# Block attention with the maxima turned later, three query slots, the next layer's norm spread into it, and gathers issued in pairs

## The reference, cut to what matters

```python
x = x + tanh(g_xattn[1]) * block_attention(layernorm(x), ctx, ctx, Wq, Wk, Wv, Wo)   # layer 2
x = x + tanh(g_ffn[1]) * hard_mixture(layernorm(x), sel_w, sel_b, comp_w, comp_b)    # layer 3
x = x + tanh(g_xattn[2]) * mlstm(layernorm(x), ctx, ctx, ..., rpe, ..., itok)        # layer 4

# block_attention: 16 heads of 8 channels, softmax over each block of 64 keys by itself
scores = einsum('bhpqd,bhpkd->bhpqk', qg, kg) * scale
attn = softmax(scores, axis=-1)
ob = einsum('bhpqk,bhpkd->bhpqd', attn, vg)
out = segment_sum(ob, rows) @ Wo.T
# layernorm(x) = (x - mean(x)) / sqrt(var(x) + 1e-5) over the channels
# hard_mixture: comp_outputs of the component whose selection logit is the largest
# mlstm: pos_emb = rpe[hops], 128 x 128 indices into a table of rows
```

## Time and profile before

| | |
|---|---|
| Median of three runs | 976.05 us (968.55 to 978.45) |
| The profiled execution | 982.52 us, its span 980.7 us |
| TensorE busy | 827.3 us (84%) |
| VectorE busy | 637.8 us (65%) |
| ScalarE busy | 555.0 us (57%) |
| GpSimd busy | 297.5 us (30%) |

### The profile page before, as it was taken

One profiled execution on the slowest core, in us unless ns is written; L12 is line 12 of the kernel. 1 busy time (PEld: TensorE's weight loads), 2 busy tenths in 40 slices (PEclk: granted clock), 3 DMA queues, 4 the chain that ended last, 5 costly groups with the idle time before them and its releaser, 6 DMA issues.

```text
span 980.7 us, 14095 instructions
## 1 busy us (share of the span) xinstructions
PE 827.3 (84%) x5561; PEld 500.1 (51%) x5569; DVE 637.8 (65%) x983; ACT 555.0 (57%) x947; POOL 297.5 (30%) x253
## 2 busy tenths in 40 slices
PE   5899999998947767789995998986889878889775
PEld 1676777774412322335544955563568754444322
DVE  3886767662566577428878667873877335776667
ACT  4797878774624344434554344444668564676464
POOL 1123332331347677433313031205792003000003
PEclk9999999997967799989995997896899998999889
DMA  6210000007000000000000000014000000000001
GB/s 223 67 65 19 24 20 21 20 23 96 14 11 15 16 19 17 20 24 22 22 14 1 1 1 1 0 44 174 0 1 1 1 1 0 1 1 0 1 0 43
DMA packets 12849, 25.65 MB, mean 26 GB/s; under 512 B 3560, under 2 KB 4848, under 8 KB 12528
## 3 DMA queue, kind: packets, MB, share of 16 engines
q1 hardware_dynamic: 8688, 16.36, 5.8%
q0 software_dynamic: 4096, 8.40, 3.4%
HBM read 23.69 MB, written 1.05 MB: 25 GB/s over the span
## 4 chain that ended last, share of the span: by engine, by line
PE 58%; DVE 24%; ACT 13%; issue 3%; DMA 1%; SPq 0%; POOL 0%; DVEq 0%; ACTq 0%
PE ps L324 8%; PE ps L296 8%; PE ps L786 6%; PE ps L925 3%; DVE small L713 3%; PE ps L561 2%; PE ps L1277 2%; PE ps L199 2%; PE ps L583 2%; DVE big L1012 2%; PE ps L1247 2%; ACT nT L218 2%; ACT nT L219 2%; DVE small L722 2%; PE ps L961 1%
## 5 line engine op out<-in xcount | busy, mean ns | idle before, releaser
L866 POOL DMA_INDIRECT pe<-in_rpe,idx x128 | 130.2, 1017 | 260.4 <-DMA pe<-in_rpe,idx 212.0
L366 DVE TENSOR_TENSOR big<-l1f_w,big 128x512 f16<-128x512 f32 x128 | 87.4, 692 | 45.1 <-ACT big L353 42.9
L352 ACT ACTIVATE l1f_w<-ps,wcols 128x512 f32<-128x512 f32 x128 | 90.0, 703 | 32.8 <-PE ps L296 30.3
L296 PE MATMUL ps<-vx,big 128*128 128x512 f16 x384 | 94.5, 399 | 2.7 <-DVE nT L225 2.7
L324 PE MATMUL ps<-big 128*128 128x128 f16 x1536 | 92.6, 221 | 4.9 <-DVE big L366 4.9
L324 PEld LDWEIGHTS ps<-big 128*128 128x128 f16 x1536 | 89.9, 99 | 12.6 <-DVE big L366 5.5
L353 ACT ACTIVATE big<-ps,wcols 128x512 f16<-128x512 f32 x128 | 90.5, 707 | 0.0
L701 ACT ACTIVATE big<-ps 128x1024 f32<-128x1024 f32 x32 | 32.7, 1023 | 60.9 <-PE ps L559 60.7
L296 PEld LDWEIGHTS ps<-vx,big 128*128 128x128 f16 x384 | 38.1, 102 | 46.4 <-issue 8.6
L786 PE MATMUL ps<-nT,l1f_w 128*128 128x512 f32 x128 | 59.3, 607 | 2.2 <-DVE nT L225 2.2
L1542 POOL TENSOR_TENSOR big<-l1f_w,big 128x512 f16<-128x512 f32 x8 | 10.1, 1267 | 138.7 <-ACT big L1579 138.7
(11 more groups left out here) (309 smaller groups left out, 1851.4 us busy)
## 6 DMA issues: line engine op xcount, KB each, us to landing
big<-in_l0x_w SPq DMA_DIRECT2D x16, 256.0 KB, 4.3
pe<-in_l2f_w SPq DMA_DIRECT2D x16, 256.0 KB, 5.8
pe<-in_rpe,idx POOLq DMA_INDIRECT x128, 2.6
cT<-in_cT SPq DMA_DIRECT2D x1, 1024.0 KB, 8.4
l1f_w<-in_l1f_w SPq DMA_DIRECT2D x1, 1024.0 KB, 5.4
vx<-in_ctok SPq DMA_DIRECT2D x1, 1024.0 KB, 16.6
out_xT<-xT SPq DMA_DIRECT2D x4, 256.0 KB, 2.2
xT<-in_xT SPq DMA_DIRECT2D x1, 768.0 KB, 6.4
```

Source lines behind the costliest of these rows:

```text
L296: mm = te.matmul(bank(f), w16[:, e, a, f * 128:(f + 1) * 128], x16[:, c, b, :], start=(n == 0), stop=(n == 2))
L352: act.activation(h32[:, f, :], bank(f), ACT.Relu, bias=b, scale=1 / W_UP)
L366: dve.tensor_tensor(h16[:, k % 2, 1, f, :], h32[:, f, :], h16[:, k % 2, 0, f, :], SUB).then_inc(M0["lo"], 1)
L866: pool.indirect_dma_start(out=pe[:, v * D:(v + 1) * D], out_offset=None, in_=ins["rpe"], in_offset=bass.IndirectOffsetOnAxis(ap=idx[:, v:v ...
```

## The change

Four things are changed.

1. In the loop of layer 2 the turning of the maxima of b+1 moves from ahead of the second pass to behind it, to the end of the batch.
2. The queries have three slots instead of two (QS = 3). The reciprocal sums `rsum` move to another buffer to make room.
3. The norm of layer 3 is taken out of `pe_norm` and its like. Chunks 0, 1 and 2 are normed within layer 2: the centring at the head of batches 6, 10 and 14 (stage 0), the variance at the head of batches 7, 11 and 15 (stage 1), on TensorE behind the same wait for the reduction as the projections; ScalarE copies, squares and takes the root, and VectorE multiplies at the end of batches 7, 11 and 15. Chunk 3 is normed in steps 0 to 2 of layer 3, in which TensorE turns no positions; the turnings of these two steps come at the end. The last output projection uses bank 3.
4. Gathers wait only once for each call, not once for each row, so that those of layer 0 and of the tail go in pairs. Eight gathers move from behind layer 2 to ahead of its first keys.

```diff
-        KS, QS = 3, 2
+        KS, QS = 3, 3
...
+        def early_at(b):
+            c, stage = divmod(b - BC - 2, BC)
+            return (c, stage) if 0 <= c < NCH - 1 and stage < 2 else (None, None)
+
+        def pe_early_norm(te, b):
+            c, stage = early_at(b)
+            if stage == 0:
+                te.wait_ge(s_x, 2 * NCH + c + 1)
+                te.matmul(bank(0), centre_w, xT[:, cs(c)], start=True, stop=True).then_inc(s_cen, 1)
+            elif stage == 1:
+                te.wait_ge(s_sq, 3 * NCH + c + 1)
+                te.matmul(bank(0), mean_w, early, start=True, stop=True).then_inc(s_var, 1)
...
+        def act_early_norm(act, link, b):
+            c, stage = early_at(b)
+            if stage == 0:
+                act.wait_ge(s_cen, 3 * NCH + c + 1)
+                act.activation(nT[:, cs(c)], bank(0), ACT.Copy)
+                act.activation(early, bank(0), ACT.Square).then_inc(s_sq, 1)
+            elif stage == 1:
+                act.wait_ge(s_var, 3 * NCH + c + 1)
+                link(act.activation(early, bank(0), ACT.Ln, bias=eps5[:]))
+                act.activation(early, early, ACT.Exp, scale=-0.5).then_inc(s_rstd, 1)
+
+        def dve_early_norm(dve, b):
+            c, stage = early_at(b)
+            if stage == 1:
+                dve.wait_ge(s_rstd, 3 * NCH + c + 1)
+                dve.tensor_tensor(nT[:, cs(c)], nT[:, cs(c)], early, MUL).then_inc(s_norm, 1)
...
+                if early_at(b)[1] is not None:
+                    if b + 1 < B:
+                        te.wait_ge(A2["mx"], 3 * b + 4)
+                    pe_early_norm(te, b)
...
                 if 1 <= b <= B:
                     pe_values(te, b - 1)
-                if b + 1 < B:
-                    pe_maxima(te, b + 1)
...
+                if b + 1 < B:
+                    pe_maxima(te, b + 1)
...
         def pool_layer2(pool, link):
+            for v in range(IN_L0, IN_L1, 2):
+                pool_gather(pool, v, v + 2)
...
-            pe_norm(te, 3)
...
+                if k == 0:
+                    te.wait_ge(s_x, 3 * NCH)
+                    te.matmul(bank(6), centre_w, xT[:, cs(NCH - 1)], start=True, stop=True).then_inc(s_cen, 1)
+                elif k == 1:
+                    te.wait_ge(s_sq, 4 * NCH)
+                    te.matmul(bank(7), mean_w, nT[:, cs(NCH - 1)], start=True, stop=True).then_inc(s_var, 1)
+                else:
+                    if k == 2:
+                        te.wait_ge(s_norm, 4 * NCH)
+                    pe_turn_positions(te, k - 2)
+            for u in (PG // 2 - 2, PG // 2 - 1):
+                pe_turn_positions(te, u)
...
         def pool_gather(pool, v0, v1):
+            if v0:
+                pool.wait_ge(s_gather, 16 * v0)
             for v in range(v0, v1):
-                if v:
-                    pool.wait_ge(s_gather, 16 * v)
```

More of the change, by code:

```diff
@@ L514, in flamingo_kernel @@
         qT = nT[:].bitcast(f16).rearrange("p (c r n) -> p c r n", c=NCH, r=2)
-        KS, QS = 3, 2
-        qblk1 = work[:, 0:1024].bitcast(f16).rearrange("p (s r j q) -> p s r j q", s=QS, r=2, j=4)
-        mblk = work[:, 1024:1536].bitcast(bf16).rearrange("p (s j q) -> p s j q", s=2, j=4)
-        rsum = work[:, 1536:2048]
+        KS, QS = 3, 3
+        qblk1 = work[:, 0:1536].bitcast(f16).rearrange("p (s r j q) -> p s r j q", s=QS, r=2, j=4)
+        mblk = work[:, 1536:2048].bitcast(bf16).rearrange("p (s j q) -> p s j q", s=2, j=4)
+        rsum = sm(1536, 512)
+        early = sm(1024, 512)
         mpart = sm(512, 32).bitcast(bf16)
@@ L582, in pe_project @@
             for j in range(4):
-                mm = te.matmul(bank(0), l1x_w[:, (3 + j) * D:(4 + j) * D], on[:, c % 2, j, :, :], start=(j == 0), stop=(j == 3))
+                mm = te.matmul(bank(3 if c == NCH - 1 else 0), l1x_w[:, (3 + j) * D:(4 + j) * D], on[:, c % 2, j, :, :], start=(j == 0), stop=(j == 3))
             mm.then_inc(A2["y_ps"], 1)
@@ L641, in pe_layer2 @@
                             te.wait_ge(s_x, 2 * NCH + (b - BC - 1) // BC + 1)
+                        c, stage = early_at(b)
+                        if stage is not None:
+                            te.wait_ge(s_sq if stage == 0 else s_rstd, 3 * NCH + c + 1)
                     for part in range(4):
@@ L668, in pool_layer2 @@
                 if b:
-                    v = IN_L0 + 2 * (b - 1)
+                    v = IN_L1 + 2 * (b - 1)
                     pool_gather(pool, v, v + 1)
@@ L679, in pool_layer2 @@
                             qT[:, b // BC, :, b % BC * S:(b % BC + 1) * S]).then_inc(A2["qblk"], 1)
-            pool_gather(pool, IN_L0 + 2 * (B - 1), S)
+            for v in range(IN_L1 + 2 * (B - 1), S, 2):
+                pool_gather(pool, v, v + 2)
         def act_queries(act, c):
@@ L698, in act_layer2 @@
                     act_queries(act, (b + 2) // BC)
+                act_early_norm(act, link, b)
                 for u in range(2):
@@ L749, in dve_layer2 @@
                     dve.wait_ge(A2["y_ps"], c + 1)
-                    dve.scalar_tensor_tensor(xT[:, cs(c)], bank(0), gt[:, 2:3], xT[:, cs(c)], MUL, ADD).then_inc(s_x, 1)
+                    dve.scalar_tensor_tensor(xT[:, cs(c)], bank(3 if c == NCH - 1 else 0), gt[:, 2:3], xT[:, cs(c)], MUL, ADD).then_inc(s_x, 1)
                 if b + 1 < B:
@@ L761, in dve_layer2 @@
                     dve_reduce(dve, b + 2, 0)
+                dve_early_norm(dve, b)
         CW2 = 2 * CW
@@ L778, in pe_layer3 @@
                 n = NC - 1 - k % NC
+                if k == 0:
+                    te.wait_ge(s_norm, 3 * NCH + 2)
+                if k == NC:
+                    te.wait_ge(s_norm, 4 * NCH)
                 for w, first_bank, done in ((n, 0, "sel"), (NC + n, 4, "comp")):
@@ L788, in pe_layer3 @@
                     mm.then_inc(F3[done], 1)
-                pe_turn_positions(te, k)
+                if k == 0:
+                    te.wait_ge(s_x, 3 * NCH)
[5 more added lines that the diff above has]
+                    if k == 2:
+                        te.wait_ge(s_norm, 4 * NCH)
+                    pe_turn_positions(te, k - 2)
+            for u in (PG // 2 - 2, PG // 2 - 1):
+                pe_turn_positions(te, u)
         def picks(k):
@@ L795, in act_layer3 @@
         def act_layer3(act, link):
-            act_norm(act, link, 3)
+            last = nT[:, cs(NCH - 1)]
             for k in range(NC * NCH // 2):
@@ L803, in act_layer3, with act_turned @@
                                bias=col("l1f_comp_b", NC - 1 - k % NC)).then_inc(F3["cand"], 1)
-                for r in range(2):
-                    act.wait_ge(X4["peT_ps"], 2 * k + r + 1)
-                    act.activation(*turned(k, r), ACT.Copy).then_inc(X4["peT_act"], 1)
+                if k == 0:
+                    act.wait_ge(s_cen, 4 * NCH)
+                    act.activation(last, bank(6), ACT.Square).then_inc(s_sq, 1)
+                elif k == 1:
+                    act.wait_ge(s_var, 4 * NCH)
+                    link(act.activation(last, bank(7), ACT.Ln, bias=eps5[:]))
+                    act.activation(last, last, ACT.Exp, scale=-0.5).then_inc(s_rstd, 1)
+                else:
+                    act_turned(act, k - 2)
+            for u in (PG // 2 - 2, PG // 2 - 1):
+                act_turned(act, u)
+        def act_turned(act, u):
+            for r in range(2):
+                act.wait_ge(X4["peT_ps"], 2 * u + r + 1)
+                act.activation(*turned(u, r), ACT.Copy).then_inc(X4["peT_act"], 1)
         def dve_layer3(dve, link):
-            dve_norm(dve, 3)
             for k in range(NC * NCH // 2):
+                if k == 2:
+                    dve.wait_ge(s_rstd, 4 * NCH)
+                    dve.tensor_tensor(nT[:, cs(NCH - 1)], bank(6), nT[:, cs(NCH - 1)], MUL).then_inc(s_norm, 1)
                 b = col("l1f_sel_b", NC - 1 - k % NC)
@@ L859, in flamingo_kernel @@
         IN_L0 = PER_STEP * NCH * E
+        IN_L1 = IN_L0 + 8
         qhalf = big[:, 0:QR * NH2 // 2 * S].rearrange("p (r j v) -> p r j v", r=QR, j=NH2 // 2)
         def pool_gather(pool, v0, v1):
+            if v0:
+                pool.wait_ge(s_gather, 16 * v0)
             for v in range(v0, v1):
-                if v:
-                    pool.wait_ge(s_gather, 16 * v)
                 pool.indirect_dma_start(out=pe[:, v * D:(v + 1) * D], out_offset=None, in_=ins["rpe"],
```

## The result

The changed kernel took 999.04 us (median of four runs, 994.83 to 1003.4), the kernel before on the same chip 975.9 us: ratio 1.025, 95% interval 1.017 to 1.033. It is slower, and by more than the upper end of the predicted range. The profiled execution took 1002.76 us, its span is 1000.9 us, against 980.7 before.

The account below looks back on a forecast made before the run. TensorE held 58% of the chain; layer 2's attention was a loop of latencies, layer 3's norm exposed. Attention +20, norm -7.3, gathers -1.6 gave +11.1 us on 976.05: 987 us, 8-in-10 range 965 to 994.

Parts of the forecast that it names:

- The port step: Layer 2 attention: a ready queries' spread on GpSimd holds VectorE's port early, so the fourth small splitting operation takes 2.61 us.
- T: Start of a batch's minus-maxima on VectorE (L730) in layer 2's attention; forecast 6.41 us after the batch's first pass starts.
- h: Start of a batch's first pass on TensorE in layer 2's attention, from which the forecast counts times.
- The fourth operation: Last of VectorE's four small splitting operations (second L723) per batch; forecast 2 us or more, ending with the queries' spread.
- the release of GpSimd by first passes alone: Layer 2: GpSimd's 6.1 us of work per batch waits for the first pass, no longer for the second.
- the place of the spreads: GpSimd, from the first pass's start: keys' spread at 0.99 to 2.89 us, queries' at 4.04 to 5.94 us.
- The norm of layer 3: Exposed norm ahead of layer 3 removed, -9.6 us; later copies before the next norm, +2.3; sum -7.3 us.
- The gathers: End of layer 1: paired, earlier gathers let the three keys' spreads start sooner, so the following norm gains 1.6 us.
- Attention: +20 us: Layer 2: batches 1 to 5 +1.9, 6 to 9 +8.9, 10 to 13 +7.2, 14 and 15 +1.8 us.
- the second rival: TensorE's clock: more waiting puts projections at 5.4 us and doubles the values, some 8 us more; 995 us, chance 0.10.
- The chance of slower: Whole kernel: 0.49, from 0.6 of the forecast and the TensorE-clock rival; slower meant above 985.8 us.
- The first rival: Fourth small operation passes, port held only while a spread runs; attention about 0, 967 us, not slower; chance 0.25.

Follow-up runs that it names:

- run 2: Kernel before with three query slots as the one change (reciprocal sums and minus-maxima moved to make room): 1002.19 us, ratio 1.0301.
- run 12: Kernel before with three query slots and GpSimd's queries' spread waiting for VectorE's four small operations: 964.99 us, ratio 0.9889.
- run 7: Changed kernel, three slots, with one wait added: GpSimd's queries' spread waits for VectorE's four small operations: 964.79 us, ratio 0.9941.
- run 8: Changed kernel with the norm of layer 3 back at its old place, three slots, no added wait: 992.19 us, ratio 1.0204.
- run 10: Changed kernel with the queries' spread waiting for VectorE's small operations and layer 3's norm at its old place: 964.5 us, ratio 0.9896.
- run 11: Changed kernel with the queries' spread waiting, scores reduced before minus-maxima in long-product batches, and layer 3's norm at its old place: 955.41 us, ratio 0.9824.
- run 5: Kernel before with one edit, the maxima turned behind the second pass; two query slots: 968.57 us, ratio 0.9987.
- run 6: Kernel before with only the norm of layer 3 moved, chunk by chunk, into the attention and layer 3's body: 977.61 us, ratio 1.0067.
- run 4: Changed kernel with 12 unused TensorE products ahead of the maxima's turning and 12 behind it, in long-product batches: 988.87 us, ratio 1.0155.
- run 1: Changed kernel with two query slots again, the rest of the change kept: 983.04 us, ratio 1.0107.
- run 9: Changed kernel with the queries' spread waiting for VectorE's small operations, and next scores reduced before the minus-maxima in long-product batches: 956.74 us, ratio 0.9823.

## Why the prediction was wrong

**Direction and place: right.** Slower, through the port.

**The port step: right.** T, the start of the minus-maxima, was to be h+6.41; it is 336.61 to 343.05, 6.44. The fourth operation, the release of GpSimd by first passes alone, and the place of the spreads came as described. That it is the ready spread, and not the slot, is shown by the pairs of runs 2 and 12 and of the change and run 7, which differ in one wait. The wait between T and a long product was to be 2.48 and is 2.47 (343.05 to 345.52).

**The norm of layer 3: -7.3 forecast, -8.7 measured** (9.77 gained, 1.06 given back). The body before had begun with a pair of products at the low clock (0.50), which hid part of the 2.8 us of later copies: in runs 2, 8, 10, 11 and 12, with the norm at its old place, the body took 70.72 us, and with it inside 73.4. By these the sum is -7.1. **The gathers: -1.6 forecast, -1.6 in the trace,** from the last L457 products of layer 1 to the norm (8.68 before, 7.04 now), below resolution alone. It depends on where the keys' spreads fall: in run 5, which issues its gathers as before, they began 2.5 us behind the start of these products instead of 0.7, and the same piece took 6.18 us. I had not seen that the transposes' slack in the kernel before was nearly used up (run 6).

**The step that failed: "Attention: +20 us". It is +36.0.** By batches, first pass to first pass:

- Start and batches 1 to 5: +4.1 instead of +1.9.
- Batches 6 to 9: 47.9 us instead of 40.95.
- Batches 10 to 13: 45.5 instead of 39.5.
- From the first pass of batch 13 to the last projection: 24.5 us, against 21.75 before: +2.7 instead of +1.8.

In batches 6 to 13 the forecast is short by 13.0 us. I had priced every long product at full clock: query 1.06, centring and variance 0.86, projection 3.63, and they took 3.72 (query and centring), 2.01, 6.51, 3.72, 2.01 and 5.33 us. The six differences are 1.80, 1.15, 2.88, 1.80, 1.15 and 1.70, together 10.5 of the 13.0. Part of the rest is the first pass and values behind them, still at the low clock: batches 8 and 12, which were to take 7.2, took 7.8 each. The remaining 1.3 us I have not traced. The same holds earlier: the projection of batch 5 took 6.65 against 5.33 before.

I had this as the second rival, with a chance of 0.10, and as an alternative to the forecast. It is no alternative: the forecast's own waits (2.2 and 2.5 us, side by side, ahead of each long product) are what lowers the clock, as run 4 shows by filling them. Its price was also too low, 8 us, since I took 5.4 us for a projection, where two of the changed kernel's took over 6.5, and counted neither queries nor norm products with it. With the waits filled, every one of these products ran at full clock. With the 16 us by which the attention exceeded my 20, the sum would have been 987 + 16 = 1003, in place of a rival at 995; the measured 999 is not told apart from that, as its interval (1.017 to 1.033) ends at 1008. The chance of slower should have been that of the port step.

**The first rival: excluded.** It decides at the fourth operation, and that took 2.61 us. Its price, 967/976 = 0.991, was near what the kernel gives where no fourth operation is held (run 7: 0.994), though not by way of two slots (run 1: 1.011).

## What to carry to other kernels

When GpSimd gets work ready earlier, look at what VectorE does in the time before that work starts: a ready two-input GpSimd instruction cost VectorE its own whole length. A wait that was there by accident can be the good part of a schedule; when you remove one, try putting it on what really must come first (here one line, 1.030 to 0.989). And price TensorE's work behind a wait that you lengthen at the low clock too (here 10.5 us in six places); a forecast that adds waits and keeps full-clock prices leaves out a cost of its own waits.

## What the runs showed of the hardware

GpSimd holds the port ahead of its record. A two-input operation of VectorE on 32 elements a partition, started while GpSimd was still issuing a gather, took 2.61 us if a spread whose semaphores were met stood next in GpSimd's queue, and 0.19 us if that spread still had a wait to pass. The hold begins at least 0.64 us before the spread's record. The Trainium skill (SBUF — State Buffer, Terms) says that VectorE and GpSimd share a port pair, locked for the full instruction, and that the loser fully blocks; the trace agrees as to the blocking, and shows it longer than the instruction's record.

It isn't all of VectorE that is blocked: in run 7 the minus-maxima, which read PSUM and SBUF, took their usual 0.69 us within a spread (350.41, the spread from 350.30 to 352.21), while a chunk product with both inputs in SBUF, begun 0.62 us before a keys' spread (352.75 and 353.37), took 3.10 us instead of 0.68. That is the same early hold, with another spread and a longer operation.

```profile
350.41 0.69 DVE L774 TENSOR_TENSOR big<-ps,consts 128x512 bf16<-128x512 f32 x1 [0.56 <-PE ps L567]
...
352.75 3.10 DVE L609 TENSOR_TENSOR nT<-nT,small 128x512 f32<-128x512 f32 x1
353.37 1.92 POOL L693 TENSOR_TENSOR big<-big,consts 128x1024 f16<-128x1024 f16 x1
```

Adding 24 useless products to each of nine batches made the kernel some 9 us faster by its ratio, and the attention 8 us shorter in the trace (run 4).

What stays open: why the clock fell in a projection behind 2.09 us of idle time in run 9 (310.27, 6.57 us) and not in another behind 2.51 us in run 7 (395.99, 3.70 us). In run 4 the last projection, whose wait of 2.10 us nothing filled, took 3.70 us, and 5.40 behind the same wait in the changed kernel and in run 7. The idle time just before doesn't decide alone.
